# Attention's queue order: a key tile's four row-maximum matmuls behind its fourth shifted score, and the copy of a unit's sums ahead of the second key tile

## The reference, cut to what matters

```python
q = (x @ wq).reshape(bsz, toks, NH, HD)
k = (x @ wk).reshape(bsz, toks, NKV, HD)
v = (x @ wv).reshape(bsz, toks, NKV, HD)
qg = q.reshape(bsz, toks, NKV, N_REP, HD)
scores = jnp.einsum('bqgrd,bkgd->bgrqk', qg, k) / jnp.sqrt(HD)
attn = jax.nn.softmax(scores.astype(jnp.float32), axis=-1)
out = jnp.einsum('bgrqk,bkgd->bqgrd', attn, v)
return out.reshape(bsz, toks, NH * HD) @ wo
```

## Time and profile before

| | |
|---|---|
| time, median of 3 runs (lowest to highest) | 852.8 us (849.96 to 853.15) |
| profiled execution: its own time | 850.92 us |
| its span in the trace | 848.9 us |
| mean granted TensorE clock | 0.989 of full speed |
| PE busy | 816.0 us (96%) |
| PE weight loads busy | 503.6 us (59%) |
| DVE busy | 622.4 us (73%) |
| ACT busy | 388.4 us (46%) |
| POOL busy | 292.1 us (34%) |

### The profile page before, as it was taken

One profiled execution on the slowest core, in us unless ns is written; L12 is line 12 of the kernel. 1 busy time (PEld: TensorE's weight loads), 2 busy tenths in 40 slices (PEclk: granted clock), 3 DMA queues, 4 the chain that ended last, 5 costly groups with the idle time before them and its releaser, 6 DMA issues. The chain is left out here.

```text
span 848.9 us, 11510 instructions
## 1 busy us (share of the span) xinstructions
PE 816.0 (96%) x4084; PEld 503.6 (59%) x4112; DVE 622.4 (73%) x804; ACT 388.4 (46%) x721; POOL 292.1 (34%) x388
## 2 busy tenths in 40 slices
PE   6999999999999999999989879999999999999995
PEld 5867433333333333333447657777777787777773
DVE  5588899999999999996036887558855795578554
ACT  4321788888888888887731022222112111122220
POOL 2212344654675465225303343342211222112221
PEclk9999999999999999999989989999999999999998
DMA  7783252344544453333225532210400040002001
GB/s 222 252 279 123 78 155 84 106 122 123 156 142 109 124 148 117 88 101 102 76 81 188 196 101 84 77 49 4 147 1 1 0 125 1 1 0 100 1 1 49
DMA packets 48224, 83.05 MB, mean 98 GB/s; under 512 B 9544, under 2 KB 13640, under 8 KB 48040
## 3 DMA queue, kind: packets, MB, share of 16 engines
q1 hardware_dynamic: 40448, 64.45, 24.5%
q0 software_dynamic: 7440, 16.76, 6.7%
q10 hardware_dynamic: 280, 1.11, 0.5%
HBM read 54.18 MB, written 28.05 MB: 97 GB/s over the span
## 5 line engine op out<-in xcount | busy, mean ns | idle before, releaser
L543 DVE TENSOR_REDUCE neg_max<-ps_pair 128x2 f32<-128x1024 f32 x256 | 301.4, 1219 | 30.6 <-PE ps_pair L641 30.6
L509 ACT ACTIVATE probs<-ps_st 128x512 f32<-128x512 f32 x512 | 265.8, 603 | 59.3 <-PE ps_st L654 58.3
L654 PE MATMUL ps_st<-q,k 50*128 50x512 f32 x512 | 185.0, 448 | 2.5 <-ACT probs L509 0.4
L654 PEld LDWEIGHTS ps_st<-q,k 50*128 50x128 f32 x512 | 83.4, 185 | 164.9 <-ACT probs L509 158.9
L892 POOL TENSOR_TENSOR g_l<-picked,g_h 128x512 fp32r<-128x512 f32 x56 | 73.0, 1303 | 250.5 <-ACT g_h L942 250.5
L641 PE MATMUL ps_pair<-k,q 48*128 48x512 f32 x512 | 149.1, 440 | 1.9 <-DVE neg_max L543 1.9
L668 PE MATMUL ps_pv<-probs,v 128*32 128x512 f32 x1024 | 136.4, 605 | 0.0
L935 ACT ACTIVATE picked<-ps_h 128x512 f32<-128x512 f32 x56 | 33.5, 598 | 182.4 <-PE ps_h L1156 182.4
L999 DVE STREAM_TRANSPOSE turned<-ps_prep 128x512 f32<-128x512 f32 x56 | 40.0, 715 | 93.3 <-PE ps_prep L1131 93.3
L1156 PE MATMUL ps_h<-xt_h,w_h 128*128 128x512 f32 x224 | 87.9, 392 | 0.5 <-ACT picked L935 0.5
L1156 PE MATMUL ps_h<-xt_l,w_h 128*128 128x512 f32 x224 | 87.5, 391 | 0.0
(11 more groups left out here) (141 smaller groups left out, 1174.6 us busy)
## 6 DMA issues: line engine op xcount, KB each, us to landing
operands<-parts POOLq DMA_DIRECT2D x20, 512.0 KB, 3.7
q<-operands SPq DMA_DIRECT2D x64, 128.0 KB, 2.5
sums<-stage SPq DMA_DIRECT2D x32, 256.0 KB, 3.1
x_raw<-xT SPq DMA_DIRECT2D x16, 256.0 KB, 5.0
k<-operands SPq DMA_DIRECT2D x64, 64.0 KB, 2.3
q<-operands SPq DMA_DIRECT2D x64, 64.0 KB, 2.6
att<-sums SPq DMA_DIRECT2D x16, 256.0 KB
yf<-x SPq DMA_DIRECT2D x4, 1024.0 KB, 5.4
```

The source lines that it names most:

```text
L509: nc.scalar.activation(probs[kt % 2][:, r], ps_st[i % 3][:], ACT.Exp, scale=float(HD) ** -0.5).then_inc(exp_done, 1)
L543: nc.vector.tensor_reduce(neg_max[:, at:at + 2], ps_max[pair % 2][:], AX.X, ALU.max, negate=True).then_inc(max_red, 1)
L654: nc.tensor.matmul(ps_st[i % 3][:], k_[n % QR][64 * a:64 * a + ROWS, kt * P:(kt + 1) * P], q[n % QR][64 * a:64 * a + ROWS, j, :], start=Tr ...
```

## The change

On PE all four row-maximum scores of a step follow shifted score 3; the three shifted scores 0, 1 and 2 then stand in a row, with `weigh` between 2 and 3 as before. On ACT the copy of the sums of unit `n - 1` moves from ahead of exponential 3 of unit `n`'s first key tile to ahead of exponential 0 of its second.

```diff
@@ ACT
                 for kt in range(TT):
                     for r in range(REP):
                         i = (n * TT + kt) * REP + r
-                        if r == 3 and kt == 0 and n:
+                        if r == 0 and kt == 1 and n:
                             take_sums(n - 1)
                         act.wait_ge(st_mm, i + 1)
@@ PE
                     ahead = 4 * step + AHEAD * TILES
                     scores_t(n, kt, 0)
                     scores_t(n, kt, 1)
-                    scores(ahead)
-                    scores(ahead + 1)
                     scores_t(n, kt, 2)
                     if step:
                         weigh(*divmod(step - 1, TT))
                     scores_t(n, kt, 3)
+                    scores(ahead)
+                    scores(ahead + 1)
                     scores(ahead + 2)
                     scores(ahead + 3)
```

## The result

The changed kernel takes 852.46 us in the median of 20 runs (850.82 to 854.78), the kernel before 851.09 us over the 20 runs timed beside it: ratio 1.0016, 95% interval 1.001 to 1.0023, so 0.9 to 2.0 us slower. The prediction had it 1.5 us faster. The time lies in the stated range, but the difference has the other sign and is 2.9 us off, and the steps show where these come from.

A forecast was written before the change was run, and what follows sets the result against it. A ring through PE and ACT at 2.61 us a step was taken to bound attention's loop. Terms -2.9 + 1.75 + 0 - 0.5 + 0.15 = -1.5 us gave 852.8 - 1.5 = 851.3 us, range 848.5 to 856.5.

The forecast's parts named there:

- The ring: Attention's unit loop: fourth shifted score, its exponential, third score, weighted sums, next fourth score set the pace, 2.61 us.
- the plain step: Attention steps without the copy or another delay were to stay at 2.61 us under PE's new order.
- DVE's wait: PE's wait for DVE before the second pair of maxima: 0.13 us to spare before the weighted sums, cost 0.
- Loads behind the stall: Rival: score weight loads show behind PE's wait for DVE, 5.5 us over 115 steps, 856.8 us; chance 0.05.
- What the old place gives back: Moving the copy from ahead of the fourth exponential saves 0.10 us once a unit, 29 times: 2.9 us.
- What the copy costs in its new place: Weighted sums behind the copy start 0.07 us late in 25 units, 1.75 us; bounds 0.05 and 0.10 each.
- The turning of the maxima: DVE's 0.20 us between two maxima once a unit shifts the second by 0.12: cost 0, upper bound 2.0 us.
- The reciprocal: Three times on DVE: weighted sums behind it 0.32 us late instead of 0.49, -0.5 us in all.
- The end of the maxima: The first output-projection matmul waits for the last maximum: +0.15 us once.
- GpSimd at 0: GpSimd takes up a unit's maxima 1.1 us later, three units before their use: cost 0.
- Nothing gained: Rival: the copy costs its full 0.10 in the new place and turning the maxima 0.07: +1.3, 854.1 us; chance 0.21.

The follow-up runs named there:

- the copy in halves: Copy of the sums cut in two, one half ahead of the fourth exponential, one behind it, PE's order as in the kernel before: 849.25 us, ratio 0.9976 to it.
- One wait: Against the change, the weighted sums of a unit's first key tile wait for the copy alone, without the exponentials' wait: 849.82 us.
- swapped waits: Against the change, both waits of the weighted sums kept, the copy's written first and the exponentials' second: 850.89 us.
- the copy's place alone: Against the kernel before, only ACT's copy moved to its new place, PE's order unchanged: 852.62 us, ratio 1.0016.
- `w1` a unit later: Against the change, GpSimd's pieces of the feed-forward weights start at unit 7, not 6: 852.52 us, ratio 1.0013 to the kernel before.
- PE's order alone: Against the kernel before, only PE's new matmul order, the copy left ahead of the fourth exponential: 853.17 us, ratio 1.003.

## Why the prediction was wrong, point by point

- **The ring, the plain step, DVE's wait: right.** Plain steps stay at 2.61 with three shifted scores behind the wait for DVE. The third score still waits for ACT, 0.32 us, so the wait for DVE costs nothing there. Loads behind the stall are not exposed: the scores' weights at 302.40 are in before ACT releases the third score at 302.91. The Trainium skill's rule (TensorE: Matmul & The Clock Gate, The mechanism) that loads overlap matmuls in flight only in another row group would have made plain steps 2.65; the traces disagree with it here.
- **What the old place gives back: right in kind, too large.** First steps fall from 2.71 to 2.61. But exponential 3 right behind the copy takes 0.59 us and not 0.60, so 0.09 of the 0.10 reached PE, and unit 29 gives nothing: its copy falls into the first step with the output projection, which takes 3.23 before and 3.23 with the copy in halves. That is 2.5 us in 28 units, and not 2.9.
- **What the copy costs in its new place: the step that failed.** I wrote "seen by PE 0.05 later: T+1.68". The 0.05 is that of a wait carried by the weight load, as the exponentials' wait is. The copy's wait stands alone: from the end of the copy to the load it takes 0.11, and the loads behind take 0.03 longer. So 0.15 and not 0.07, outside my upper bound of 0.10, in 25 units 3.8 us and not 1.75. One wait and swapped waits bring it to 0.06, and the copy's place alone shows that it is no matter of PE's order.
- **The turning of the maxima: right.** The second maximum starts 0.12 to 0.13 behind it, and the steps behind it take 2.61.
- **The reciprocal: right.** Its delay is 0.32 in place of 0.49, and the copy's 0.15 hides beneath:

```profile
198.21 0.18 PEld L654 LDWEIGHTS ps_st<-q,k 50*128 50x128 f32 x1 [0.84 <-ACT probs L509]
...
199.25 0.18 PEld L641 LDWEIGHTS ps_pair<-k,q 48*128 48x128 f32 x2 [0.75 <-DVE neg_max L543]
...
200.14 0.16 PEld L668 LDWEIGHTS ps_pv<-probs,v 128*32 128x32 f32 x8 [0.36 <-issue]
201.13 0.18 PEld L654 LDWEIGHTS ps_st<-q,k 50*128 50x128 f32 x1 [0.84 <-ACT probs L509]
```

  The bank is seen free at T+1.04, the weighted sums go at T+1.93, as worked out from the earlier trace rows.
- **The end of the maxima: right.** The first output-projection matmul starts 0.56 behind its T instead of 0.43, and the step takes 3.34 instead of 3.23, +0.11 (+0.12 to +0.14 in the other runs with the new order).
- **GpSimd at 0: wrong.** I wrote "three units before their use". The maxima of a unit are ready three units ahead, but the DMA that brings them to `q` is issued in GpSimd's unit before. In unit 6, where GpSimd is busy or waits for its own piece of `w1` throughout, maxima that come 1.1 us later were enough to make it late: 0.78 us once, and nothing with `w1` a unit later.
- The sum with the measured terms: -2.5 + 3.8 - 0.5 + 0.1 + 0.8 = +1.7, against +1.41 in the loop and +1.4 in the medians. The other 0.3 is rounding and steps that are some thousandths of a microsecond shorter in this trace. Of the 2.9 us between -1.5 and +1.41 the copy's wait is 2.1, GpSimd 0.8 and the old place 0.4. "Nothing gained" had the right size, and of its two causes the first in kind: the weighted sums are 0.12 late behind the copy. The second, the turning of the maxima, cost nothing.
- I also put the difference on a median of three runs, 852.8, that stands 1.7 us above the 851.09 of twenty. This hid in the predicted time what the difference shows.

## What to carry to other kernels

Where a change makes another semaphore the last of several to end, look at which wait the instruction carries and which stands alone; write first, or alone, the one that will end last. A short operation that fits nowhere whole may fit free in two parts, each within the idle time of its own place. And when an engine off the path gets its input later, ask for its next deadline in its fullest stretch, not for how far ahead its result is used.

## What the runs showed of the hardware that I had not expected

- With the wait for the copy as an instruction of its own, PE's weight load starts 0.11 us after the copy ends (the change and the copy's place alone), against 0.05 with that wait on the load (one wait, waits swapped), and the eight loads take 0.19 instead of 0.16 us.
- Of two waits written ahead of a matmul in these kernels the first was on the load and the second stood alone; swapping them swapped that.
- The duration of an exponential depends on its place in a chain without gaps: 0.60 us behind a gap, then 0.59, 0.60, 0.62 and 0.63, the second starting 0.49 behind the first and each further one 0.48 behind its forerunner (medians, before and PE's order alone). The fifth of such a chain ends 0.03 later than its start lets one expect.
